# Attention and feed-forward sandwich on one core: one low sum behind the first exponentials, the last store on ScalarE's queue, two slices of the last block in other PSUM banks, and a new order of the engines' programs

## The chip, the core and the metric

The kernel runs on one core of a Trainium2 chip. Its engines run programs of their own and meet through semaphores: TensorE (PE; PEld is its weight load), VectorE (DVE), ScalarE (ACT), GpSimd (POOL), and SyncE (SP), which here only issues DMAs. The metric is the device time of one execution in microseconds (us); lower is better.

## What is computed

The input is x with 8 batches of 256 tokens of 128 features. Two residual steps follow each other, both with a layer norm ahead of and behind the inner function:

```
x = x + layernorm(attention(layernorm(x)))
x = x + layernorm(ffn(layernorm(x)))

attention: q, k, v = x Wqkv; softmax(q k^T / sqrt(128)) v          # one head of 128
ffn:       h = silu(x W1 * s1) * (x W2 * s2)                       # 128 -> 512
           h = gelu(h H1 * s3); h = gelu(h H2 * s4)                # 512 -> 512, twice
           y = h W3 * s5                                           # 512 -> 128
```

The weights of the ffn are -1, 0 or 1; s1 to s5 are scales of one output column each. All is float32.

## The kernel before

The 2048 tokens are 16 tiles of 128. They go through in five blocks of 2, 4, 4, 4 and 2 tiles (SIZES), blocks 0 to 4; the last is called LAST. Tokens stand along the free dimension in the ffn, so a slice (o = 0 to 3) is 128 of the 512 hidden features by all tokens of a block (256 or 512 columns).

**Steps of a block.** Attention: x_statistics, x_normalised (VectorE), x_transposes (TensorE), xT_copy; g_projection and scores (the product of q and k goes through one matrix "qk"); maxima (VectorE), exps (ScalarE, L382), probs_transposes (L1065), pT_copy, attend (L1081); then attention_out, x1_block, x1_normalised (VectorE). Each statistics step is followed by rsqrt on GpSimd (L315), which makes 1/std (rstd) of one of four norms, LN_X, LN_O, LN_X1, LN_Y. Ffn: x2_transposes; x2T_high (ScalarE) and x2T_low (VectorE) split the transposed input into a rounded high half and a low rest; up_high and up_low (L1121, L1128) are the two products with W1 and W2; silu (ScalarE) and gate (VectorE, L724) make the first activation; high and low (VectorE, L732, L621) split it. The layers are named A1, A2, A3 by the activation that they read: A1 multiplies by H1, A2 by H2, A3 by W3. gelu_high (L436) and gelu (L428) on ScalarE write the high half and the full activation of the next layer, low (VectorE) the low half. The last layer is followed by scaled_yT, y_transposes, y_statistics, y_shifts, y_normalised, last_add (GpSimd) and the store. The last block's last layer is written by another way: last_down (L1197), last_statistics (L770), rsqrt_last (L321), last_centred, last_out (L783), and a store per tile (L267).

**Begin and end.** A layer's products on TensorE are written as begin(layer, block, slices, early) and end(...): begin waits until the slices' PSUM banks are free (bank_free) and does the products of the first `early` input slices, high and low; end does the rest. high_terms and low_terms wait slice by slice for the high and low halves.

**PSUM.** There are eight banks, F0 to F3 and A0 to A3. The hidden layers write slice o into F[o]; up products of the last block use A0 to A3; attention uses the A banks (the F banks in block 0).

**Low sums and flags.** The weights are loaded twice, raw by SP (w12_raw, h1_raw, h2_raw, w3_raw) and rounded by a casting DMA of GpSimd (w12_hi, h1_hi, h2_hi, w3_hi; round_w12 and so on). low_sum(0) to low_sum(5) add up the low 16 bits of the raw weights to learn whether rounding lost anything: 0 (w12_raw) and 1 (h1_raw) on ScalarE (L461), 2 to 5 (h1_raw, h2_raw, h2_raw, w3_raw) on VectorE (L793). sum_flags (L993) sums them over partitions on TensorE, copy_flags (L799) puts the result into SBUF, and read_flag reads it into a register of TensorE, which decides at each slow_branch whether extra products are needed. With these weights they aren't. Flag 0 covers W1, W2 and half of H1, flag 1 the rest.

**What sets the order.** Each engine's program is a list of calls written out by hand at the end of its function: it runs its steps exactly in that order, and a step that waits holds up all behind it. SP's queue holds, in this order: x of block 0, the attention weights, x of block 1, the scales, x of block 2, w12_raw, h1_raw, h2_raw, x of block 3, w3_raw, x of block 4, then the stores. The lines that the change's first part touches, in ScalarE's list:

```
v_copy(0)
low_sum(0)
exps(0, 0)
xT_copy(1)
w3_row_copy()
gT_copy(1)
low_sum(1)
```

## Time and profile before

| | us |
|---|---|
| median of 3 runs | 131.22 (130.95 to 131.62) |
| the profiled execution | 130.89 |
| its span, from the first to the last instruction | 128.7 |
| TensorE busy | 121.8 (95%) |
| VectorE busy | 103.9 (81%) |
| ScalarE busy | 97.5 (76%) |
| GpSimd busy | 28.0 (22%) |

The spans are read on the slowest (here the only) core. A matmul's end is modelled, and matmuls overlap by some 0.16 us, so the start of a row's successor says more of the pace than a row's duration. The first 12 us and the last 4 us are where TensorE is least busy.

### The profile page before, as it was taken

The numbers are of one execution on the slowest core, as the hardware profiler recorded it, in microseconds if no ns is written. First come the engines' busy times: TensorE is split into PE (matmuls) and PEld (weight loads), VectorE is DVE, ScalarE is ACT, GpSimd is POOL, SyncE is SP. The second block draws the span as 40 slices with busy tenths as digits, with TensorE's granted clock in tenths as the row PEclk, the third lists the DMA queues.
The fourth block names the chain that finished last, engine by engine and source line by source line (L and its number), as shares of the span: only waits on it lengthen the run. The fifth ranks groups of instructions, "written<-read, shape, count | busy, mean of one in ns | idle before, by whom it ended". The sixth has DMA issues, their size and how long they took to land.

```text
span 128.7 us, 2354 instructions
## 1 busy us (share of the span) xinstructions
PE 121.8 (95%) x698; PEld 102.2 (79%) x698; DVE 103.9 (81%) x337; ACT 97.5 (76%) x182; POOL 28.0 (22%) x40
## 2 busy tenths in 40 slices
PE   7994999999999999999999999999999999999980
PEld 5582979999777988887889888888888778789970
DVE  1693789999998899966799999839999977696843
ACT  3237699987999929399999289799992996996520
POOL 3390330035300015410000084400002540000351
PEclk9999999999999999999999999999999999999999
DMA  4779999000300000000000001010000011000021
GB/s 105 234 248 399 383 376 341 21 0 8 81 0 5 0 0 8 0 0 0 5 0 0 0 5 41 26 58 3 0 5 0 0 44 43 0 5 0 0 76 52
DMA packets 5343, 8.28 MB, mean 64 GB/s; under 512 B 464, under 2 KB 2768, under 8 KB 5328
## 3 DMA queue, kind: packets, MB, share of 16 engines
q1 hardware_dynamic: 3984, 5.19, 12.5%
q0 software_dynamic: 1344, 2.88, 6.9%
q8 instruction: 10, 0.16, 0.5%
q14 instruction: 5, 0.04, 0.1%
HBM read 7.02 MB, written 1.05 MB: 63 GB/s over the span
## 4 chain that ended last, share of the span: by engine, by line
PE 79%; DMA 5%; ACT 5%; DVE 4%; issue 2%; SPq 2%; POOL 1%; POOLq 1%; ACTq 0%; DVEq 0%
PE F L1168 20%; PE F L1174 20%; PE A L1081 5%; PE A L1049 5%; DMA w_raw<-w 5%; PE F L1128 4%; PE F L1121 4%; PE A L1168 3%; PE A L1174 3%; PE A L1032 2%; PE A L1065 2%; PE A L1020 2%; ACT a_hi L436 2%; ACT act_full L428 1%; PE A L1209 1%
## 5 line engine op out<-in xcount | busy, mean ns | idle before, releaser
L315 POOL TENSOR_TENSOR rstd<-mv,minus_half 128x4 f32<-128x4 f32 (+1 forms) x19 | 18.4, 968 | 90.9 <-DVE mv L628 90.8
L1168 PE MATMUL F<-a_hi,h_hi 128*128 128x512 f32 (+1 forms) x160 | 37.1, 354 | 0.1
L1174 PE MATMUL F<-a_lo,h_hi 128*128 128x512 f32 (+1 forms) x160 | 36.4, 349 | 0.0
L621 DVE TENSOR_TENSOR a_lo<-act_full,a_hi 128x512 fp32r<-128x512 f32 (+1 forms) x52 | 31.1, 615 | 5.6 <-ACT act_full L428 4.5
L436 ACT ACTIVATE a_hi<-F,sc 128x512 fp32r<-128x512 f32 (+1 forms) x35 | 21.4, 625 | 13.5 <-PE F L1174 13.5
L1174 PEld LDWEIGHTS F<-a_lo,h_hi 128*128 128x128 f32 x160 | 26.7, 189 | 4.2 <-DVE a_lo L621 0.4
L1168 PEld LDWEIGHTS F<-a_hi,h_hi 128*128 128x128 f32 x160 | 26.3, 189 | 3.9 <-ACT act_full L428 0.5
L428 ACT ACTIVATE act_full<-F,sc 128x512 f32<-128x512 f32 (+1 forms) x40 | 24.0, 613 | 1.7 <-PE F L1174 1.7
L724 DVE SCALAR_TENSOR_TENSOR act_full<-F,sc,silu 128x512 f32<-128x512 f32 (+1 forms) x16 | 10.7, 677 | 0.6 <-ACT silu L417 0.5
L417 ACT ACT_TABLE_LOAD x8 | 10.3, 1283 | 0.1
L417 ACT ACTIVATE silu<-F,sc 128x512 f32<-128x512 f32 (+1 forms) x16 | 9.8, 634 | 0.5 <-PE F L1128 0.3
L1121 PE MATMUL F<-x2T_hi,w_hi 128*128 128x512 f32 (+1 forms) x32 | 10.1, 396 | 0.1
L1128 PE MATMUL F<-x2T_lo,w_hi 128*128 128x512 f32 (+1 forms) x32 | 9.4, 376 | 0.0
L628 DVE BATCH_NORM_AGGREGATE mv<-stats 128x2 f32<-128x9 f32 x62 | 8.1, 170 | 0.0
L732 DVE CAST a_hi<-act_full 128x512 fp32r<-128x512 f32 (+1 forms) x17 | 6.5, 392 | 1.2 <-ACT act_full L428 1.0
L631 DVE BATCH_NORM_STATS2 stats<-A 128x6 f32<-128x128 f32 x28 | 6.6, 277 | 0.0
L1121 PEld LDWEIGHTS F<-x2T_hi,w_hi 128*128 128x128 f32 x32 | 5.3, 189 | 1.3 <-issue 0.5
L1128 PEld LDWEIGHTS F<-x2T_lo,w_hi 128*128 128x128 f32 x32 | 5.5, 188 | 0.9
L631 DVE BATCH_NORM_STATS2 stats<-xs 128x6 f32<-128x128 f32 x16 | 3.8, 277 | 3.1 <-DMA xs<-x 3.1
L337 POOL TENSOR_TENSOR outs<-y_n,x 128x512 f32<-128x512 f32 (+1 forms) x4 | 4.6, 1160 | 5.7 <-ACT y_n L451 3.8
L644 DVE TENSOR_SCALAR xn<-x,mv,rstd 128x128 f32<-128x128 f32 x16 | 5.5, 404 | 0.3 <-POOL rstd L315 0.3
L684 DVE TENSOR_REDUCE neg_max<-A 128x2 f32<-128x512 f32 x7 | 4.7, 677 | 0.8 <-PE A L1049 0.7
(153 smaller groups left out, 192.0 us busy)
## 6 DMA issues: line engine op xcount, KB each, us to landing
h_raw<-h SPq DMA_DIRECT2D x2, 1024.0 KB, 11.5
h_hi<-h POOLq DMA_DIRECT2D x2, 1024.0 KB, 9.5
xs<-x SPq DMA_DIRECT2D x3, 256.0 KB, 3.6
out<-outs SPq DMA_DIRECT2D x3, 256.0 KB, 2.1
w_raw<-w SPq DMA_DIRECT2D x1, 512.0 KB, 6.2
w_hi<-w POOLq DMA_DIRECT2D x1, 512.0 KB, 7.7
xs<-x SPq DMA_DIRECT2D x2, 128.0 KB, 8.5
w_raw<-w SPq DMA_DIRECT2D x1, 256.0 KB, 15.7
```

The costliest lines, as they stand in the source:

```text
L315: nc.gpsimd.tensor_tensor(rstd[:, ln, tiles(b)], mv[:, ln, tiles(b), 1], minus_half[:, 0:SIZES[b]], ALU.pow).then_inc(rstd_ready[ln], 1)
L417: nc.scalar.activation(silu1[:, o % 2, c], up_banks(b, o)[0][:, c], ACT.Silu, scale=sc[:, S_W1 + o:S_W1 + o + 1]).then_inc(silu_ready, 1)
L428: nc.scalar.activation(act_full[:, o, c], F[o][:, c], ACT.Gelu, scale=sc[:, s:s + 1]).then_inc(a_full[n], 1)
L436: nc.scalar.activation(a_hi[n][:, o, c], F[o][:, c], ACT.Gelu, scale=sc[:, s:s + 1]).then_inc(a_hi_ready[n], 1)
L621: nc.vector.tensor_tensor(dst, full, hi.bitcast(f32), ALU.subtract).then_inc(done, 1)
L628: return nc.vector.bn_aggr(mv[:, ln, T0[b] + t, :], stats[:, ln, T0[b] + t, :])
L631: nc.vector.bn_stats(stats[:, ln, T0[b] + t, 0:6], tile(t)).then_inc(chain, 1)
L724: nc.vector.scalar_tensor_tensor(gated(b)[:, o, c], up_banks(b, o)[1][:, c], sc[:, S_W2 + o:S_W2 + o + 1], silu1[:, o % 2, c], ALU.mult, A ...
L1121: nc.tensor.matmul(bank, w_hi, x_hi, start=True, stop=False)
L1128: last = nc.tensor.matmul(bank, w_hi, x_lo, start=False, stop=True)
L1168: nc.tensor.matmul(out, terms[k][0], terms[k][2], start=(k == 0), stop=False)
L1174: last = [nc.tensor.matmul(out, terms[k][0], terms[k][3], start=False, stop=(k == KT - 1)) for out, terms in groups]
```

## The change

1. On ScalarE low_sum(0) moves behind exps(0, 0) and xT_copy(1). 2. The last tile's store moves from SP's queue to ScalarE's, with a semaphore of its own. 3. The last block's first two slices of layer A1 are written into A0 and A1 and no longer into F0 and F1; bank_free follows. 4. The five lists are in a new order; sums of work on each engine stay as they are.

```diff
+        def layer_bank(n, b, o):
+            if n == A1 and b == LAST and o < 2:
+                return A[o]
+            return F[o]
...
-            def store_last(t):
-                g, j = G0[LAST] + t // 2, t % 2
-                sp.wait_ge(last_ready, t + 1)
-                sp.dma_start(out_view[:, g, j * D:(j + 1) * D], outs[:, T0[LAST] + t, :]).then_inc(out_stored, 16)
+            def store_first_of_last():
+                sp.wait_ge(last_ready, 1)
+                sp.dma_start(out_view[:, G0[LAST], 0:D], outs[:, T0[LAST], :]).then_inc(out_stored, 16)
...
-            sp.wait_ge(out_stored, 16 * (LAST + SIZES[LAST]))
+            sp.wait_ge(out_stored, 16 * (LAST + 1))
+            sp.wait_ge(last_stored, 16)
...
             round_h1()
+            round_h2()
+            round_w3()
             rsqrt(LN_O, 0)
-            round_h2()
             rsqrt(LN_X1, 0)
             rsqrt(LN_O, 1)
             rsqrt(LN_X1, 1)
-            round_w3()
             rsqrt(LN_X, 3)
+            rsqrt(LN_X, 4)
             rsqrt(LN_O, 2)
             rsqrt(LN_Y, 0)
+            last_add(0)
             rsqrt(LN_X1, 2)
-            rsqrt(LN_X, 4)
             rsqrt(LN_O, 3)
             rsqrt(LN_Y, 1)
-            last_add(0)
...
-                nc.scalar.activation(act_full[:, o, c], F[o][:, c], ACT.Gelu, scale=sc[:, s:s + 1]).then_inc(a_full[n], 1)
+                nc.scalar.activation(act_full[:, o, c], layer_bank(n - 1, b, o)[:, c], ACT.Gelu, scale=sc[:, s:s + 1]).then_inc(a_full[n], 1)
...
+            def store_second_of_last():
+                act.wait_ge(last_ready, 2)
+                act.dma_start(out_view[:, G0[LAST], D:2 * D], outs[:, T0[LAST] + 1, :]).then_inc(last_stored, 16)
...
-            low_sum(0)
+            w3_row_copy()
             exps(0, 0)
             xT_copy(1)
-            w3_row_copy()
+            low_sum(0)
             gT_copy(1)
...
             y_statistics(0)
-            low(A2, 1, 0)
-            x1_block(2)
-            low(A2, 1, 1)
             low(A2, 1, 2)
             low(A2, 1, 3)
             y_shifts(0)
+            x1_block(2)
+            low(A3, 1, 0)
             x1_normalised(2)
...
             last_statistics(0)
+            last_statistics(1)
             last_centred(0)
-            last_statistics(1)
+            last_centred(1)
             last_out(0)
-            last_centred(1)
             last_out(1)
...
             def bank_free(n, b, slices):
                 if n == A1:
                     for o in slices:
-                        if b == LAST:
+                        if b == LAST and o < 2:
+                            pe.wait_ge(a_full[A1], KT * b + 3)
+                        elif b == LAST:
                             pe.wait_ge(a_full[A3], KT * (b - 1) + o + 1)
...
                 elif n == A2:
                     for o in slices:
                         pe.wait_ge(a_full[A2], KT * b + o + 1)
+                        if b == LAST and o < 2:
+                            pe.wait_ge(a_full[A3], KT * (b - 1) + o + 1)
```

**ScalarE in the head.** The rows are the start of its program, with the tensor that each writes and reads; low_bits from w12_raw is low_sum(0), the two act_full, sums rows are exps(0, 0). Before:

```order
L374 ACTIVATE act_full<-F1 128x256
L374 ACTIVATE act_full<-F2 128x256
L461 ACTIVATE low_bits,low_sums<-w12_raw 128x1024
L382 ACTIVATE act_full,sums<-F3,neg_max 128x256 x2
L374 ACTIVATE xT_odd<-A1 128x512
L475 ACTIVATE w3_row<-A3 128x128
L374 ACTIVATE gT_odd<-A1 128x512
L461 ACTIVATE low_bits,low_sums<-h1_raw 128x1024
```

And now:

```order
L475 ACTIVATE w3_diag<-ident,sc 128x128
L378 ACTIVATE act_full<-F2 128x256
L479 ACTIVATE w3_row<-A3 128x128
L386 ACTIVATE act_full,sums<-F3,neg_max 128x256 x2
L378 ACTIVATE xT_odd<-A1 128x512
L465 ACTIVATE low_bits,low_sums<-w12_raw 128x1024
L378 ACTIVATE gT_odd<-A1 128x512
L465 ACTIVATE low_bits,low_sums<-h1_raw 128x1024
```

The low sum has moved behind the exponentials and block 1's xT copy, and the small w3 steps stand elsewhere.

**TensorE around the second flag.** F0 and F1 from a1_hi and a1_lo are the first two slices of layer A1 of block 0; A2 from xT_even is scores(2, 1); the TENSOR_LOAD is read_flag. Before, the second one stood behind all of the layer's products:

```order
L993 MATMUL A1<-low_sums,ones 1x3
L1049 MATMUL A2<-xT_even,gT_even 128x256 x2
L1168 MATMUL F0<-a1_hi,h1_hi 128x256
L1168 MATMUL F1<-a1_hi,h1_hi 128x256
L1092 COMPARE_AND_BRANCH
...
L1174 MATMUL F3<-a1_lo,h1_hi 128x256 x4
L998 TENSOR_LOAD flags
L1168 MATMUL F0<-a2_hi,h2_hi 128x256
```

Now it stands ahead of the last input slice of the first two:

```order
L1002 MATMUL A1<-low_sums,ones 1x3
L1058 MATMUL A2<-xT_even,gT_even 128x256 x2
L1007 TENSOR_LOAD flags
L1181 MATMUL F0<-a1_hi,h1_hi 128x256
L1181 MATMUL F1<-a1_hi,h1_hi 128x256
L1101 COMPARE_AND_BRANCH
```

The read has moved some twenty products forward.

**VectorE ahead of the last block's first layer.** a1 rows are the last block's first activation (kept in pT_odd), a3 rows block 3's last; each CAST is high, each TENSOR_TENSOR is low. Before:

```order
L732 CAST a3_hi<-act_full 128x512
L621 TENSOR_TENSOR a3_lo<-act_full,a3_hi 128x512
L621 TENSOR_TENSOR a1_lo<-pT_odd,a1_hi 128x256
L732 CAST a1_hi<-pT_odd 128x256
L621 TENSOR_TENSOR a1_lo<-pT_odd,a1_hi 128x256
L621 TENSOR_TENSOR a3_lo<-act_full,a3_hi 128x512 x3
```

And now:

```order
L741 CAST a3_hi<-act_full 128x512
L741 CAST a1_hi<-pT_odd 128x256
L630 TENSOR_TENSOR a1_lo<-pT_odd,a1_hi 128x256
L630 TENSOR_TENSOR a3_lo<-act_full,a3_hi 128x512
L630 TENSOR_TENSOR a1_lo<-pT_odd,a1_hi 128x256
L630 TENSOR_TENSOR a3_lo<-act_full,a3_hi 128x512 x3
```

The first low half of block 3's last activation has moved behind one high and one low half of the last block. On ScalarE, gelu(A3, 3, 0), which the first CAST reads, now stands behind gelu_high(A3, 3, 1).

## Rows read from the trace of the kernel before

**Rows 1.** One stretch: length, busy us of each engine (instructions), PEclk, DMA share, GB/s.

```profile
38.00:50.00 12.00, 12.00 (x70) 10.18 (x69) 10.64 (x31) 9.16 (x15) 2.02 (x2) 1.00 0.01 3
```

**Rows 2.** TensorE's longest wait: engine, line, waited for: us in total, times, longest.

```profile
PE F L1065 <- ACT act_full L382: 1.6, 1, 1.6
```

**Rows 3.** The chain that ended last: start us, us, what.

```profile
3.10 6.22 DMA w_raw<-w
9.35 1.15 ACT low_bits L461 x2
...
28.23 0.14 ACT a_hi L436
...
37.69 1.16 PE A L1081 x8
```

**Rows 4.** In order of time, VectorE and ScalarE to 28 us: start, us, instruction [idle].

```profile
8.37 0.69 DVE L684 TENSOR_REDUCE neg_max<-F 128x2 f32<-128x512 f32 x1
...
10.41 0.46 ACT L382 ACTIVATE act_full<-F,neg_max 128x256 f32<-128x256 f32 x1
...
18.39 0.69 DVE L793 SCALAR_TENSOR_TENSOR low_pairs<-h_raw 128x512 bf16<-128x512 uint16 x1
...
19.00 0.14 DVE L799 TENSOR_REDUCE flags<-F 1x1 f32<-1x3 f32 x1
...
21.05 0.42 DVE L793 SCALAR_TENSOR_TENSOR low_pairs<-w_raw 128x256 bf16<-128x256 uint16 x1 [0.22 <-DMA w_raw<-w]
...
27.30 0.42 DVE L621 TENSOR_TENSOR a_lo<-act_full,a_hi 128x256 fp32r<-128x256 f32 x1
```

**Rows 5.** Line L276, the load of h2_raw: its issue, and its time to landing.

```profile
L276 SPq DMA_DIRECT2D h_raw<-h x1: 507/507/507, 4.1 to 4.1; - x1
...
DMA to landing us min/median/max: 14.2/14.2/14.2
```

**Rows 6.** In order of time, TensorE's weight loads and matmuls at two places.

```profile
19.82 0.42 PEld L1065 LDWEIGHTS A<-ident,probs_odd 128*128 128x128 f32 x4 [0.21 <-issue]
...
27.91 0.40 PE L1174 MATMUL F<-a_lo,h_hi 128*128 128x256 f32 x2
```

**Rows 7.** GpSimd's rsqrt(LN_O, 0), and its two h loads with the times to landing.

```profile
14.92 0.71 POOL L315 TENSOR_TENSOR rstd<-mv,minus_half 128x2 f32<-128x2 f32 x1 [5.24 <-DVE mv L628]
...
L305 POOL DMA_DIRECT2D h_hi<-h x1: 797/797/797, 8.9 to 8.9; - x1
L308 POOL DMA_DIRECT2D h_hi<-h x1: 778/778/778, 15.6 to 15.6; - x1
...
DMA to landing us min/median/max: 8.0/9.5/10.9
```

**Rows 8.** Near 104 us, VectorE and GpSimd in order of time; the page's group of L621.

```profile
104.12 1.32 DVE L621 TENSOR_TENSOR a_lo<-act_full,a_hi 128x512 fp32r<-128x512 f32 x1 [0.66 <-ACT act_full L428]
...
103.58 1.30 POOL L337 TENSOR_TENSOR outs<-y_n,x 128x512 f32<-128x512 f32 x1 [1.43 <-ACT y_n L451]
...
L621 DVE TENSOR_TENSOR a_lo<-act_full,a_hi 128x512 fp32r<-128x512 f32 (+1 forms) x52 | 31.1, 615 | 5.6 <-ACT act_full L428 4.5
```

**Rows 9.** Near 113 us, TensorE and VectorE in order of time.

```profile
111.80 1.07 PE L1174 MATMUL F<-a_lo,h_hi 128*128 128x512 f32 x4
113.00 0.95 PE L1168 MATMUL F<-a_hi,h_hi 128*128 128x256 f32 x6
...
113.71 0.42 DVE L621 TENSOR_TENSOR a_lo<-pT_odd,a_hi 128x256 fp32r<-128x256 f32 x1
```

**Rows 10.** The tail, VectorE, GpSimd and SP's queue in order of time.

```profile
125.21 0.29 DVE L770 BATCH_NORM_STATS2 stats<-F 128x6 f32<-128x128 f32 x1
...
125.81 0.60 POOL L321 TENSOR_TENSOR rstd<-mv,minus_half 128x1 f32<-128x1 f32 x1 [0.26 <-DVE mv L771]
...
126.02 1.15 SPq L267 DMA_DIRECT2D out<-outs  x2
```

**Rows 11.** The page: GB/s of all DMAs in 40 slices of 3.2 us.

```profile
GB/s 105 234 248 399 383 376 341 21 0 8 81 0 5 0 0 8 0 0 0 5 0 0 0 5 41 26 58 3 0 5 0 0 44 43 0 5 0 0 76 52
```

157 lines of the change are left out of this document (79 added, 78 removed).

## The prediction

> **What bounds the kernel now.** I read a table by stretch of time first, then what TensorE waited for, then the chain that ended last, and last the engines' own rows at the places where that chain leaves TensorE. In a stretch such as 38 to 50 us TensorE is busy all of the time, at full clock [rows 1]: there, instructions of other engines are hidden unless they come so late that TensorE has to stand. Time can be had at four places only. (1) The head: the longest wait of a matmul is 1.6 us, for the first exponentials (PE L1065 behind ACT L382) [rows 2]. The chain says why: w12_raw, issued at 3.10, lands 6.22 us later; only then does ScalarE's first low sum run, from 9.35 for 1.15 us [rows 3]; the exponentials stand behind it. (2) At 104 us products wait for a late low half (a_lo). (3) At 112.7 us the last block's first hidden layer stands until 113.00. (4) The tail behind TensorE's last matmul.
>
> **The head, step by step.** The maxima of batch 0 are ready at 8.37 + 0.69 = 9.06, but the exponentials start at 10.41, behind the low sum [rows 4]. Turned round, they start at about 9.1: 1.3 us earlier. TensorE also gets x_transposes(2) into the wait that is left, which saves it some 0.4 us behind. By its own list TensorE could be 1.7 us ahead. It doesn't keep this. VectorE's low_sum(3) reads h2_raw, which was issued at 4.1 and took 14.2 us to land [rows 5], so it lands at 18.3. In the trace of before low_sum(3) starts at 18.39 [rows 4], hardly later; after the change VectorE gets there sooner and stands until 18.3, and x2T_low(0), without which up_low(0, 0) can't run, is queued behind it. From there to low(A1, 0, 3), the step at 27.30 [rows 4], VectorE is full in both orders. It gains 18.39 to 18.32 (0.07), the 0.22 us wait for w3_raw at 21.05, as that sum moves back behind the first gates, and copy_flags(0), 0.14 us at 19.00, which moves ahead of the landing [rows 4]. Sum 0.43: low(A1, 0, 3) starts at 26.87.
>
> Then there is the second flag. read_flag(1) moves from behind all of A1's end groups to ahead of the first, right behind scores(2, 1). Before, many products were queued in TensorE when it read. Now all that is queued ends near 26.7, and copy_flags(1), which now comes behind high(A1, 0, 3), ends at about 26.75 too, just ahead of low(A1, 0, 3). What such a read costs is seen at the first flag: it was written at 19.00 + 0.14 = 19.14 [rows 4], and the next weights loaded at 19.82 after an idle 0.21 us with no engine named for it, "issue" [rows 6]. That is 0.68 us, the price I take. TensorE goes on at 26.75 + 0.68 = 27.43 with 2 high products (0.24), and at 27.67 come the 2 low ones that stood at 27.91 [rows 6]. So the first Gelu of layer 2, at 28.23 in the chain [rows 3], comes 0.24 earlier or a little more; I take 0.3. The range is 0.24 to 0.75: the latter if the read is hidden after all, for then VectorE's 0.43 and the 0.3 by which TensorE was later than VectorE here both count. From 28.23 to the attend at 37.69 [rows 3] the chain runs over ScalarE, VectorE and GpSimd in turn, through the same instructions in both orders: maxima(2, 1) only changes places with x_normalised(3), and the pT copy behind both comes no later. So the gain is handed on. **Head: -0.3 us.**
>
> **From 38 to 103 us.** I followed each moved step there to its use by TensorE. The closest are x1_block(2), now behind y_shifts(0) and so about 2 us later, whose normalised tiles come some 0.5 us before x2_transposes(2) wants them, and low(A1, 3, 3), with next to nothing to spare. No stall and no gain: **0**, range 0 to +0.4. On GpSimd the two weight loads (0.78 us for h2) fill part of the 5.24 us for which it idled before rsqrt(LN_O, 0) at 14.92 [rows 7]: 4 us of cover, cost 0. w3_diagonal behind gT_copy(0) is still ahead of its product: 0.
>
> **104 us.** gelu(A2, 3, 2) goes ahead of the four y_n. The low half made from it started at 104.12 and took 1.32 us, beside GpSimd's add of 1.30 us from 103.58; the mean of that line is 615 ns [rows 8]. Now two other low halves stand ahead of it and the add comes later too, since its y_n do, so that both start near 104.15: it ends between 104.8 and 105.5, and TensorE wants it near 105.4. Gain between 0.3 and 0; against it, x1_normalised(4) comes before a low half instead of behind it and waits for GpSimd's rstd, up to 0.1. **-0.1.**
> The Trainium skill (SBUF — State Buffer, Who interferes with whom) says that VectorE and GpSimd share a pair of ports which whoever starts first may hold for its whole instruction. By that rule the 1.32 us holds a wait, and the trace agrees. By it the moved last_add(0) could also hold up x1_block(2) or x1_normalised(2) by its whole length, some 0.8 us: TensorE would lose 0.3 us, and the sum below would be 0.6 instead of 0.9.
>
> **111 us.** The last 4 low products of layer 2 of block 3 start at 111.80; 4 of 0.23 end at 112.71. The next start at 113.00, when gelu(A3, 3, 1) has emptied F1 [rows 9]. In A0 and A1 they need only gate(4, 2), long done. Behind them 6 + 6 + 2 products of 0.12 lead to the low ones of the last slice at 114.39, for which low(A1, 4, 3) must be there; it ended at 113.71 + 0.42 = 114.13 [rows 9]. high(A3, 3, 0), ahead of it, now waits for a Gelu that stands second on ScalarE, one Gelu step or 0.6 us later; 0.3 to 0.4 of this is made good since low(A1, 4, 2) now runs where low(A3, 3, 0) stood waiting. So it ends at 114.3 to 114.45: just in time. Gain 0.29, and 0.06 for uneven starts after a stop: **-0.35**, range -0.4 to 0 (if VectorE is 0.35 late).
>
> **Tail.** The second tile's statistics start at 125.21 behind last_centred(0); now they start as soon as TensorE is done, at 125.05. Its rstd on GpSimd, at 125.81, then starts and ends 0.15 earlier, and last_out(1), which waits for it, starts 0.13 earlier [rows 10]. The store on ScalarE's queue buys nothing: SP's two issues lie within 126.02 to 127.17 [rows 10]; the second came due near 126.8, when the first had been handed over. What a first use of another queue costs is in no row; nearest is SP's issue itself, so I bound it at -0.1 to +0.35 and take 0. **-0.13.**
>
> **Sum**: -0.3 - 0.1 - 0.35 - 0.13 = -0.88. The profiled execution took 130.89 (span 128.7, and 2.2 around it): 130.0 after. The median of the runs is 131.22, 0.33 higher; medians are compared, so I forecast 131.22 - 0.9 = 130.3.
>
> **Rivals.** (a) *The flag's read is hidden*: -0.75 in place of -0.3, so 129.8. Against it: the 0.68 us at the first flag. (b) *A new stall in the middle, or a late low(A1, 4, 3)*, takes back 0.4 us or more: 130.7 to 131.2. For it: margins of 0 to 0.5 us at three places. (c) *The other side: the cast loads crowd out h2_raw.* The issue of h2_hi moves from 15.6 [rows 7] to 9.7 and w3_hi follows right behind, while h2_raw is under way, on whose landing VectorE hangs. They are 1.25 MB, 3.2 us at the 376 to 399 GB/s of those slices [rows 11]. If they are served side by side with h2_raw, it slips by s, up to 3.2 us, and the time is 130.3 + s: slower than before from s = 0.9, and 133.5 at the end. For it: between 10 and 22 us no bandwidth is left [rows 11]. Against it: the two h loads of GpSimd, issued at 8.9 and 15.6, took 10.9 and 8.0 us [rows 7], so the first lands at 19.8 and the second, which by then had been waiting, at 23.6: one after the other. h2_hi issued at 9.7 stands behind h1_hi as it did before.
> The Trainium skill (DMA: Bandwidth & Descriptors, Queues, rings and completion order) says that each DMA engine takes turns between queues, packet by packet, and starts the descriptors of one queue in order. By that rule h2_raw keeps its share whatever stands behind h1_hi, s is 0, and the sum stands; no trace here shows four such loads in one queue.
>
> **Chances.** Forecast 0.5 (130.3, own range 129.9 to 130.7), (a) 0.13, (b) 0.27, (c) 0.1. Some 0.66 us (0.5%) is what a measurement of this kernel can tell from none. Faster by more: (a) and most of the forecast's 0.5, 0.56. Slower by more: (c) beyond s = 1.6 and the worst of (b), 0.11. Same: 0.33. The range 129.5 to 131.5 holds (a), the forecast, (b), and (c) while s is small.
>
> **What would show it.** Exponentials of batch 0 at 9.1; VectorE idle until 18.3 before low_sum(3), ended by a DMA; TensorE idle for some 0.7 us near 27 us, named "issue"; first Gelu of layer 2 near 27.9; attend(2, 0) near 37.4; no matmul gap ahead of the last block's first layer. A landing of h2_raw past 19 us, or a TensorE wait over 0.3 us between 38 and 103, would prove me wrong.

## The result, and the profile after

| | before | changed |
|---|---|---|
| median of 20 runs each, us | 130.16 (129.68 to 131.62) | 129.91 (129.43 to 130.88) |
| profiled execution, us | 130.89 | 130.00 |
| its span, us | 128.7 | 127.8 |
| w12_raw, issue to landing in it, us | 6.2 | 6.4 |
| h2_raw, the same | 14.2 | 13.9 |

The ratio of the runs is 0.9943, with a 95% interval of 0.9919 to 0.9968: 0.42 to 1.05 us faster, at the middle 0.74 us. The means of the 20 runs stand 0.55 apart (130.45 and 129.91), the medians only 0.25, against the 0.9 forecast, for the reason below. The forecast was 130.3 us after a gain of 0.9; the gain of the two profiled executions is 0.89. Whether it exceeds 0.5% the interval doesn't settle. Runs above 132 us, with a granted clock of 0.98 to 0.99, are left out of all that follows, the profiled execution of the fourth kernel of experiment 3 among them.

**Two levels of time, which the three first runs hid.** The 20 runs of the kernel before are 11 between 129.68 and 130.19 us, and 9 between 130.73 and 131.62, with nothing between (in the later sets some runs fall into the gap). The three runs behind the 131.22 of the prediction are all of the upper group, and so is the profiled execution. Over all its runs of this study, the kernel before has 104 below 130.35 us (median 129.8) and 85 between 130.35 and 131.62 (130.9); a median between such groups tells of their shares. Of the changed kernel's 20 runs, 18 are below 130.35.

**The head.** In the changed kernel, in order of time, first the start of the chain that ended last, then VectorE's and ScalarE's instructions to 28 us (start, us, instruction, and in brackets the idle time before it and what ended it):

```profile
2.64 3.86 DMA xs<-x
...
8.69 0.60 DVE neg_max L693
```

```profile
9.32 0.47 ACT L386 ACTIVATE act_full<-F,neg_max 128x256 f32<-128x256 f32 x1 [0.38 <-DVE neg_max L693]
...
17.05 0.15 DVE L808 TENSOR_REDUCE flags<-F 1x1 f32<-1x3 f32 x1
17.99 0.69 DVE L802 SCALAR_TENSOR_TENSOR low_pairs<-h_raw 128x512 bf16<-128x512 uint16 x1 [0.21 <-DMA h_raw<-h]
...
26.21 0.14 DVE L808 TENSOR_REDUCE flags<-A 1x1 f32<-1x3 f32 x1
26.39 0.43 DVE L630 TENSOR_TENSOR a_lo<-act_full,a_hi 128x256 fp32r<-128x256 f32 x1
...
27.46 0.47 ACT L440 ACTIVATE a_hi<-F,sc 128x256 fp32r<-128x256 f32 x1 [0.49 <-PE F L1187]
```

The chain no longer begins with the landing of w12_raw [rows 3]: it begins with the x of the second group. The exponentials run at 9.32 in place of 10.41 [rows 4], and what is left before them is VectorE's maximum. low_sum(3) now stands until h2_raw has landed, as forecast, but at 17.99, not 18.3, since h2_raw took 13.9 us here in place of 14.2 [rows 5]. The idle time there is 0.21 us, and experiment 7 shows that nothing behind it would have come earlier without it. The first flag's copy, at 19.00 before, is at 17.05. The first Gelu of layer 2 comes at 27.46 in place of 28.23: 0.77 earlier, where 0.3 was forecast.

**The second flag and the middle.** TensorE's weight loads and matmuls of the changed kernel at five places:

```profile
26.73 0.30 PEld L1181 LDWEIGHTS F<-a_hi,h_hi 128*128 128x128 f32 x2 [0.21 <-issue]
...
36.85 1.16 PE L1090 MATMUL A<-v_even,pT_even 128*128 128x128 f32 x8
...
38.57 0.30 PEld L1130 LDWEIGHTS F<-x2T_hi,w_hi 128*128 128x128 f32 x2 [0.36 <-issue]
...
107.34 0.30 PEld L1130 LDWEIGHTS A<-x2T_hi,w_hi 128*128 128x128 f32 x2 [0.47 <-issue]
...
122.22 1.95 PE L1210 MATMUL F<-w_scaled,act_full 128*128 128x128 f32 x16
```

The flag's copy ended at 26.35 and the next weights are loaded at 26.73: 0.38 us, of which only 0.21 is idle, as products were still running at the copy's end; and not 0.68. attend(2, 0) starts at 36.85, 0.84 before the 37.69 of [rows 3]. TensorE's last products start at 122.22; before:

```profile
123.06 1.95 PE L1197 MATMUL F<-w_scaled,act_full 128*128 128x128 f32 x16
```

That is again 0.84. So from 37 to 122 us nothing was gained: 85.37 us lie between the two marks in both kernels. There were gains on the way, and they were spent. The loads at 38.57 (up_high(1, 3), which now waits for gate(1, 1)) and at 107.34 (up_high(4, 2)) stand 0.36 and 0.47 us where those of before stood 0 and 0.26. Most of the loss is early: attend(2, 1) starts 4.60 or 4.61 us after attend(2, 0) in the changed kernel, in all its profiles that have this order, and 4.43 to 4.45 in those with the old order.

GpSimd's last_add(0), which the change moves forward, meets a small instruction of VectorE, o_shift, that stood alone and took 0.15 us before:

```profile
53.78 0.74 POOL L341 TENSOR_TENSOR outs<-y_n,x 128x256 f32<-128x256 f32 x1 [2.47 <-ACT y_n L455]
53.81 0.73 DVE L713 TENSOR_TENSOR o_shift<-mv,rstd 128x4 f32<-128x4 f32 x1
```

It takes 0.73 us in seven of the ten profiles of kernels with the new order, and 0.15 in three, where the add takes 0.79 or 0.80 instead. In the first kind TensorE's load of x2T_hi near 59 us starts 22.64 to 22.66 us after attend(2, 0), in the second 22.54 to 22.58 (without the edit of up_high(1, 3)): some 0.1 us, which is still there at the last products (85.25 to 85.37 and 85.14 to 85.21).

**104 and 111 us.** VectorE and GpSimd near 104 us, then TensorE and VectorE near 112 us, in the changed kernel:

```profile
102.19 1.89 DVE L630 TENSOR_TENSOR a_lo<-act_full,a_hi 128x512 fp32r<-128x512 f32 x3
105.44 0.68 DVE L630 TENSOR_TENSOR a_lo<-act_full,a_hi 128x512 fp32r<-128x512 f32 x1
...
103.57 1.67 POOL L341 TENSOR_TENSOR outs<-y_n,x 128x512 f32<-128x512 f32 x1 [2.00 <-ACT y_n L455]
```

```profile
111.25 1.07 PE L1187 MATMUL F<-a_lo,h_hi 128*128 128x512 f32 x4
112.16 0.88 PE L1181 MATMUL A<-a_hi,h_hi 128*128 128x256 f32 x6
...
113.33 0.42 DVE L630 TENSOR_TENSOR a_lo<-pT_odd,a_hi 128x256 fp32r<-128x256 f32 x1
```

The low half of 1.32 us [rows 8] is gone: three take 1.89 together, and it is GpSimd's add that is now longer, 1.67 for 1.30. The high products of the last block's first layer follow the low ones of block 3's layer A2 without a stop, and its low half, which was to end between 114.3 and 114.45, ends at 113.75: VectorE wasn't late.

**The tail.** VectorE, GpSimd and the two queues, in the changed kernel:

```profile
124.21 0.30 DVE L779 BATCH_NORM_STATS2 stats<-F 128x6 f32<-128x128 f32 x1
...
124.15 1.23 POOL L325 TENSOR_TENSOR rstd<-mv,minus_half 128x1 f32<-128x1 f32 x2 [0.64 <-DVE mv L780]
...
125.51 0.34 SPq L271 DMA_DIRECT2D out<-outs  x1
...
125.80 0.37 ACTq L483 DMA_DIRECT2D out<-outs  x1
```

The second tile's rstd follows the first with no gap on GpSimd (0.26 us of idle before it in [rows 10]). last_out(1) ends at 125.76, 3.54 us after TensorE's last products began, where it was 3.73 before: 0.19 gained, 0.13 forecast. But from TensorE's last products to the end of the execution it is 7.78 us (7.76 to 7.78 in all nine profiles with the store on ScalarE's queue) after 7.83 (7.82 to 7.85 in the old order): only some 0.06 is left.

### The profile page after: what moved, and what is told of

Its sections match the earlier page's. It is cut to its first block, busy times and chain, and to the rows that moved or that the text cites. A ratio compares the mean times of both kernels' runs of the same rounds, so it can differ in the third digit from the quotient of the medians.

```text
span 127.8 us, 2356 instructions
## 1 busy us (share of the span) xinstructions
PE 122.6 (96%) x698; PEld 102.5 (80%) x698; DVE 103.3 (81%) x337; ACT 97.4 (76%) x182; POOL 27.9 (22%) x40
## 3 DMA queue, kind: packets, MB, share of 16 engines
q1 hardware_dynamic: 3840, 5.12, 12.6%
HBM read 7.02 MB, written 1.05 MB: 63 GB/s over the span
## 4 chain that ended last, share of the span: by engine, by line
PE 84%; DVE 6%; DMA 3%; ACT 1%; SPq 1%; issue 1%; DVEq 0%; ACTq 0%
PE F L1181 22%; PE F L1187 22%; PE A L1090 5%; PE A L1058 5%; PE F L1130 5%; PE F L1137 5%; PE A L1187 3%; PE A L1181 3%; DMA xs<-x 3%; PE A L1041 3%; PE A L1074 2%; PE A L1029 2%; DVE xn_odd L653 2%; PE F L1210 1%; PE A L1222 1%
## 5 line engine op out<-in xcount | busy, mean ns | idle before, releaser
L319 POOL TENSOR_TENSOR rstd<-mv,minus_half 128x4 f32<-128x4 f32 (+1 forms) x19 | 17.7, 935 | 87.1 <-DVE mv L637 87.0
L1181 PE MATMUL F<-a_hi,h_hi 128*128 128x512 f32 (+1 forms) x152 | 35.5, 355 | 0.0
L630 DVE TENSOR_TENSOR a_lo<-act_full,a_hi 128x512 fp32r<-128x512 f32 (+1 forms) x52 | 30.6, 602 | 5.9 <-ACT act_full L432 5.2
L1187 PE MATMUL F<-a_lo,h_hi 128*128 128x512 f32 (+1 forms) x152 | 34.9, 352 | 0.0
L440 ACT ACTIVATE a_hi<-F,sc 128x512 fp32r<-128x512 f32 (+1 forms) x33 | 20.5, 632 | 12.2 <-PE F L1187 12.2
L1187 PEld LDWEIGHTS F<-a_lo,h_hi 128*128 128x128 f32 x152 | 25.7, 189 | 4.0
L1181 PEld LDWEIGHTS F<-a_hi,h_hi 128*128 128x128 f32 x152 | 25.2, 189 | 3.6 <-issue 0.2
L432 ACT ACTIVATE act_full<-F,sc 128x512 f32<-128x512 f32 (+1 forms) x38 | 23.1, 621 | 1.7 <-PE F L1187 1.7
L341 POOL TENSOR_TENSOR outs<-y_n,x 128x512 f32<-128x512 f32 (+1 forms) x4 | 5.1, 1274 | 9.1 <-ACT y_n L455 6.9
```

The source lines that it names most:

```text
L319: nc.gpsimd.tensor_tensor(rstd[:, ln, tiles(b)], mv[:, ln, tiles(b), 1], minus_half[:, 0:SIZES[b]], ALU.pow).then_inc(rstd_ready[ln], 1)
L432: nc.scalar.activation(act_full[:, o, c], layer_bank(n - 1, b, o)[:, c], ACT.Gelu, scale=sc[:, s:s + 1]).then_inc(a_full[n], 1)
L440: nc.scalar.activation(a_hi[n][:, o, c], layer_bank(n - 1, b, o)[:, c], ACT.Gelu, scale=sc[:, s:s + 1]).then_inc(a_hi_ready[n], 1)
L630: nc.vector.tensor_tensor(dst, full, hi.bitcast(f32), ALU.subtract).then_inc(done, 1)
L1181: nc.tensor.matmul(out, terms[k][0], terms[k][2], start=(k == 0), stop=False)
L1187: last = [nc.tensor.matmul(out, terms[k][0], terms[k][3], start=False, stop=(k == KT - 1)) for out, terms in groups]
```

## Experiments

**1. The two kernels again, together on another chip.** No edit.

> The kernel before, once more, to see the spread of its own times and a second profile of it. Before's 20 times lie in two groups, 129.7 to 130.3 and 130.7 to 131.6; the profile that the prediction was built on is of the second (130.89). Theory (one level, the spread is the chip's): a second profile has the same gaps as the first (1.6 us before the first exponentials, 0.3 us at 113 us), whatever its time, and span 127.5 to 129. Rival (the gap at the head is itself variable, by the landing of w12_raw or h2_raw): in a profile with a time near 129.8 the first Gelu of layer 2 comes near 27.2, and in one near 130.9 near 28.2. Ratio to before 1.000, within 0.3%.

> The changed kernel, once more. Theory (the sum of the prediction, -0.9 us of 130 to 131): ratio 0.993. Rival (the true effect is the -0.25 us by which the two medians of 20 differ): ratio 0.998.

Before: median 129.98 us of 12 runs. Changed: 129.74 of 12, ratio 0.9974 (0.9941 to 1.0007). The profiled execution of before took 129.92 this time, 0.97 less than the first one of the same program. The load of w12_raw in it, its issue and its time to landing:

```profile
L274 SPq DMA_DIRECT2D w_raw<-w x1: 468/468/468, 3.1 to 3.1; - x1
...
DMA to landing us min/median/max: 4.8/4.8/4.8
```

and ScalarE and VectorE in it, in order of time:

```profile
7.91 1.06 ACT L461 ACTIVATE low_bits<-w_raw 128x1024 bf16<-128x1024 uint16 x1 [0.45 <-DMA w_raw<-w]
...
9.49 0.47 ACT L382 ACTIVATE act_full<-F,neg_max 128x256 f32<-128x256 f32 x1 [0.43 <-DVE neg_max L684]
...
17.50 0.69 DVE L793 SCALAR_TENSOR_TENSOR low_pairs<-h_raw 128x512 bf16<-128x512 uint16 x1
...
27.32 0.84 ACT L436 ACTIVATE a_hi<-F,sc 128x256 fp32r<-128x256 f32 x2 [0.61 <-PE F L1174]
```

The same load, issued at the same 3.1 us, lands 4.8 us later in place of 6.2 [rows 3]. The low sum is over before the maxima are, and the wait of 1.6 us [rows 2] isn't there: the exponentials wait for VectorE, low_sum(3) waits for nothing, and the first Gelu is 0.91 us earlier than in [rows 3]. So most of what the prediction calls the head's limit exists in one kind of execution only. Of the five profiles of kernels that keep VectorE's sums on their loads and before's order of VectorE and TensorE in the head (before twice, the two of experiment 2 and the first of experiment 3), the two with late landings lie in their kernel's upper group and the three with early ones in the lower. Over the 20 profiles taken for this study the load takes 4.5 to 4.9 us in 8 and 5.9 to 6.5 us in 12, never between, and h2_raw 11.4 to 12.6 us in the first and 13.4 to 14.4 in the second. With early landings the changed kernel gains less: its profile of this set (129.35 us; 4.5 and 12.6) is 0.57 below that of before, with attend(2, 0) 0.40 earlier and the last products 0.50.

But these 0.40 us aren't the change's. The exponentials start at 9.08 in this profile and at 9.49 in that of before, 0.41 apart, and from there to attend(2, 0) it is 27.29 and 27.28 us. In the 12 profiles whose chain begins with the load of the second group of x, the load takes 3.68 to 4.18 us and the exponentials start 2.82 or 2.83 us after its landing, whichever kernel it is. Two more profiles of the new order with early landings, in experiments 7 and 3, start the exponentials at 9.31 and 9.30 and take 130.04 (0.13 of it by its store) and 129.85 us, which is no less than the 129.67 to 129.92 of the old order with early landings (experiments 1, 2 and 3). Counted from the first exponential to the last products, the old order without a wait for w12_raw takes 112.52 to 112.78 us and the new one 112.50 to 112.83 (112.90 with late landings). So with early landings the change is worth some 0.1 us, and most of that is the tail.

**2. The banks alone, and the low sum alone.** The kernel before with layer_bank, which puts two slices of A1 of the last block into A's banks (as in the change's diff), and the kernel before with low_sum(0) behind xT_copy(1):

```
 exps(0, 0)
 xT_copy(1)
+low_sum(0)
```

> The kernel before with the last block's first two A1 slices in A0 and A1 (and what waits for these banks), and nothing else. Theory: the 0.3 us stop of TensorE before that layer goes, as in the changed kernel, so -0.3 us, ratio 0.998, and the matmuls there follow at 112.7. Rival: VectorE's low halves, which are in the old order here, are late and a stop of the same size stands a few products further on: 0.

> The kernel before with low_sum(0) behind exps(0, 0) and xT_copy(1) on ScalarE, and nothing else: all other orders are before's. Theory (VectorE hangs on the landing of h2_raw near 18.1): exponentials 1.1 to 1.3 us earlier, but low_sum(3) can start only 0.1 to 0.3 us earlier, so the first Gelu of layer 2 comes 0.2 to 0.4 us earlier, and the time is 0.3 us less, ratio 0.998. Rival (the head's 1.3 us is handed on whole): first Gelu near 27.0, ratio 0.991.

Banks: 5 runs at 129.09 to 129.38 and 7 at 130.05 to 130.68 us. Both levels of before, 129.46 to 130.2 and 130.72 to 131.28 beside it, have moved down by some 0.4 to 0.6 us. The median of 130.13 and the ratio of 0.9992 (0.9956 to 1.0027) hide that, since 7 of 12 runs fell in its upper group and only 12 of 34 of before's. Its TensorE rows, three marks in order of time:

```profile
37.46 1.16 PE L1086 MATMUL A<-v_even,pT_even 128*128 128x128 f32 x8 [0.19 <-DVE pT_even L665]
...
111.49 1.07 PE L1183 MATMUL F<-a_lo,h_hi 128*128 128x512 f32 x4
112.39 0.88 PE L1177 MATMUL A<-a_hi,h_hi 128*128 128x256 f32 x6
```

No stop at 112.4, as forecast, and the last products start at 122.38, 84.92 us after attend(2, 0), 0.45 less than in the first profile of either kernel and 0.37 to 0.45 less than in all with the old order (85.29 to 85.37). So the banks are worth some 0.4 us, a little more than the -0.35 of the prediction, and the new order of the middle takes nearly as much away (85.14 to 85.37 with both).

The low sum alone: 5 runs at 129.67 to 129.94, two at 130.21 and 130.40, 5 at 130.76 to 131.18; median 130.30, ratio 1.0025 (0.9989 to 1.0061). Both groups stay. Taking the load off the first exponentials isn't enough by itself.

**3. Are the loads the cause?** Six sums wait for loaded tiles. Their input is replaced by a constant tensor: for n = 0 only, for all six, for all six in the changed kernel, and for VectorE's four only. The flags then say nothing of the weights' low words.

```
-act.wait_ge(loaded, 16)
+act.wait_ge(zeroed, 4)
+half_words = spare.unsqueeze(1).to_broadcast([P, 8, P])
```

> The kernel before, in its old order, but low_sum(0) adds up the low bits of a constant tensor of ones (same columns, same engine) and waits for no load; so W1 and W2 are left out of the check for lost bits. Theory A (the two groups of before's times are two landings of the weight loads, about 7.9 and 9.3 us for w12_raw, and low_sum(0) hands on only the late one): the first low sum runs near 7.5 in every run and the exponentials at 9.5; in the late state low_sum(3) still waits for h2_raw (18.3), so 0.3 to 0.4 of the 0.9 us go and the upper group moves from 130.9 to 130.5 while the lower stays at 129.8. Rival B (the upper group comes from low_sum(0)'s wait alone): no upper group, all times 129.5 to 130.1, ratio 0.995. Rival C (the two groups have nothing to do with these loads): both groups stay, ratio 1.000.

> The kernel before, in its old order, with all six low sums on a constant tensor of ones, so no engine's program waits for a raw weight load except w3_scale near the end (the check for lost bits is left out altogether). Theory A: no upper group, 129.5 to 130.0 in all runs, since neither low_sum(0) nor low_sum(3) hands on a late landing; ratio 0.995 to 0.997. Rival C: both groups stay (130.7 to 131.2 in a third of the runs), ratio 1.000.

> The changed kernel with all six low sums on a constant tensor of ones (the check for lost bits is left out). Theory A: the changed kernel waits only for h2_raw before low_sum(3), by 0.2 us in the late state; its times go from 129.2 to 130.4 to 129.1 to 129.6, ratio 0.995 to before. Against e6 it then shows what the change is worth without any load in play: -0.3 to -0.5 us. Rival (the head's new order is worth 0.9 us by itself): 0.9 us under e6.

> The kernel before with the four sums that VectorE takes (n = 2 to 5) over a constant tensor in place of the loaded tiles; ScalarE's two (n = 0, 1) still wait for theirs. So the flags no longer stand for the tiles' words. Theory A (VectorE's sum over h2_raw, which ended at 18.39 us beyond the wait for the landing, and hangs back the second head's scores, makes the upper group): hardly any run above 130.5 us, median 129.8 to 130.0, as with all six sums off the loads. Theory B (the upper group comes from ScalarE's sums over w12_raw and h1_raw ahead of and behind the first exponentials): a third to two thirds of the runs stay at 130.6 to 131.4 us, and the median lies at 130.2 to 130.7. In a profile with the late landings A expects the first Gelu of layer 2 at 27.3 us, B at 27.9 or later.

With n = 0 off, 6 of 12 runs stay above 130.8; with VectorE's four off, 3 of 11 above 130.7 and two at 130.31 and 130.47 (of before, 20 of 35 beside it). With all six off, 10 of 12 are below 130.2 (median 129.88, ratio 0.9948, 0.9915 to 0.9981), and its profile shows late landings (6.0 and 13.4 us) beside early marks, in order of time:

```profile
9.32 0.47 ACT L382 ACTIVATE act_full<-F,neg_max 128x256 f32<-128x256 f32 x1 [0.78 <-DVE neg_max L692]
...
17.33 0.69 DVE L809 SCALAR_TENSOR_TENSOR low_pairs<-ones_sq 128x512 bf16<-128x512 uint16 x1
...
27.28 0.84 ACT L436 ACTIVATE a_hi<-F,sc 128x256 fp32r<-128x256 f32 x2 [0.61 <-PE F L1190]
```

27.28 is the 27.32 of an early execution. So late loads do no harm unless a sum waits for them, and the sum over w12_raw isn't the only one that does: without its wait the upper group stays. Whether ScalarE's two sums alone make one is less clear, since 3 to 5 of 11 is not much more than the 2 of 12 with all six off; what the first of them costs is seen in experiment 5. The changed kernel with all six off has a median of 129.79, 0.09 below: without late loads in play, the change is worth a tenth, as the profiles of experiment 1 say.

**4. The loads pushed later on purpose.** One more load, ahead of that of w12_raw:

```
+sp.dma_start(spare_raw[:, :], w3).then_inc(spare_loaded, 16)
 sp.dma_start(w12_raw[:, :], w12).then_inc(w12_loaded, 16)
```

> The kernel before with one more load, the 0.25 MB of w3 into a tile that nobody reads, on SP's queue ahead of w12_raw's. At the 376 to 399 GB/s of the head that is 0.7 us, by which w12_raw, h1_raw and h2_raw land later. Theory A (late landings make the upper group, and each 0.1 us of lateness beyond 7.9 us at w12_raw costs 0.1 us): the lower group goes away; all runs above 130.3 us, median 130.9 to 131.7. Theory B (the groups have another cause, and the landings only go with it): both groups stay where they are, 129.5 to 130.2 and 130.5 to 131.6 us.

> The changed kernel with the same further load of 0.25 MB ahead of w12_raw's. Theory A (the changed kernel has the first exponentials off the load and waits for h2_raw alone, which costs it little up to a landing at 18.3 us): median 129.9 to 130.6 us, 0.2 to 0.8 above that without the load, and 0.7 us or more below that of the kernel before with the same load. Theory B (the lateness costs both the same): it stays 0.2 to 0.4 us below the kernel before with the same load, in a profile with the same landings.

Before with it: one run at 130.21, the ten others from 130.54 to 131.74, median 130.91 us, where the kernel before had 17 of 22 below 130.35 beside it. The lower group is gone. ScalarE in its profile:

```profile
9.76 1.06 ACT L465 ACTIVATE low_bits<-w_raw 128x1024 bf16<-128x1024 uint16 x1 [2.23 <-DMA w_raw<-w]
10.82 0.46 ACT L386 ACTIVATE act_full<-F,neg_max 128x256 f32<-128x256 f32 x1
```

The changed kernel with it: 130.22, 0.69 lower, 8 of 12 below 130.35. This settles that late landings raise the time of before, and that the changed kernel bears them better. It isn't immune: 4 runs lie at 130.83 to 131.77, and its profiled one (131.16) was late from wa_raw on, which took 3.25 us to land.

**5. Single moves of the head undone or made alone.** In the changed kernel: low_sum(0) ahead of the first exponentials; copy_flags(0) behind low_sum(3); low_sum(4) right behind low_sum(3); up_high(1, 3) behind up_low(1, 2); and that together with low_sum(3) behind pT_copy(1, 0). As diffs to the changed kernel, in this order:

```
+low_sum(0)
 exps(0, 0)
 xT_copy(1)
-low_sum(0)
...
-copy_flags(0)
 x1_normalised(0)
 low_sum(3)
+copy_flags(0)
...
 low_sum(3)
+low_sum(4)
 x2T_low(0)
 pT_copy(1, 0)
-low_sum(4)
...
-up_high(1, 3)
 up_low(1, 2)
+up_high(1, 3)
...
-low_sum(3)
 x2T_low(0)
 pT_copy(1, 0)
+low_sum(3)
```

> The changed kernel with low_sum(0) back ahead of the first exponentials. Theory A (the move behind the exponentials is what took the upper group away): an upper group comes back, a third or more of the runs at 130.2 to 131.0 us, median 129.9 to 130.3. Theory B (the move is worth next to nothing by itself, and the new order of the second head's work took the upper group away): median 129.7 to 129.9, no run or one above 130.3. In a profile with the late landings the exponentials begin at 10.3 us under both, and the first Gelu of layer 2 at 27.9 to 28.2 under A, 27.5 under B.

> The changed kernel with copy_flags(0) back behind low_sum(3) on VectorE, where a late h2_raw holds it. Theory A (the first flag's copy behind the sum over h2_raw is the second of two waits that make the upper group: TensorE can't read the flag until it is copied): with h2_raw landing late the copy is at 19.0 us and the first Gelu of layer 2 at 27.9 to 28.2 us, as in the kernel before; a third or more of the runs at 130.3 to 131.0 us, the median 129.9 to 130.4. Theory B (the sum's own wait matters, not what stands behind it; the changed kernel has the same wait): median 129.7 to 129.9 us, first Gelu at 27.4 to 27.6.

> The changed kernel with low_sum(4) back between low_sum(3) and x2T_low(0) on VectorE. Theory A (what matters is only that the flag's copy is ahead of the late sum): median 129.7 to 129.9 us as without the edit. Theory B (0.68 us of low_sum(4) ahead of x2T_low(0), on which up_low(0, 0) waits, is what binds, and more so when h2_raw is late): the head comes 0.5 to 0.7 us later in a profile with the late landings, median 130.1 to 130.5 us.

> The changed kernel with up_high(1, 3) behind up_low(1, 2) again, as in the kernel before. In the changed kernel's trace its weights load after an idle 0.36 us at 38.2 to 38.6, since it waits for gate(1, 1), which ends at 38.46. Theory: that stop goes (up_low(1, 2) stands in it), 0.2 us less at the attend of 41.6 and at the end, time of e2 less 0.2 us. Rival: TensorE's stop only moves on to up_high(1, 3) behind: 0.

> The changed kernel with up_high(1, 3) back behind up_low(1, 2), and with low_sum(3) behind x2T_low(0) and pT_copy(1, 0) on VectorE, so that a late h2_raw holds back one read of a flag and nothing else at the head. Theory A (what is left of h2_raw's landing is on the path in the changed kernel): the head gains 0.2 to 0.5 us in the profile with the late landings and 0 to 0.2 with the early ones, median 129.4 to 129.6 us. Theory B (the flag's read then comes later and takes the gain back, since low_sum(3) has to end before copy_flags(1) and moves by the 1 us of the two copies): median 129.7 to 129.9 us, the same as without the edit.

| edit to the changed kernel | median us | ratio to before (95%) | first Gelu of layer 2 in the profile | the same, counted from the first exponential |
|---|---|---|---|---|
| none (20 runs, and 12) | 129.91, 129.74 | 0.9943, 0.9974 | 27.46, 26.98 | 18.14, 17.90 |
| low_sum(0) ahead | 130.75 | 1.0027 (0.9990 to 1.0064) | 28.28 | 17.72 |
| copy_flags(0) behind | 131.04 | 1.0069 (1.0041 to 1.0098) | 29.02 | 19.46 |
| low_sum(4) ahead | 130.54 | 1.0026 (0.9995 to 1.0057) | 28.00 | 18.36 |
| up_high(1, 3) behind | 129.68 | 0.9920 (0.9892 to 0.9948) | 27.61 | 18.30 |
| that, and low_sum(3) behind | 130.43 | 0.9992 (0.9959 to 1.0026) | 28.06 | 18.79 |

All profiles but the 26.98 have the late landings. By the medians, three moves are each worth 0.6 to 1.3 us here, though low_sum(0) made alone in the kernel before was worth nothing. In the profiles, low_sum(4) costs 0.22 us from the first exponential on; the rest of its later Gelu is a later x. The lowest runs of the three, 130.10, 130.59 and 130.04 us, lie above the changed kernel's medians: either nearly all of their runs were late, or the moves also count when the loads land early. No early profile of them was taken, so this stays open. low_sum(0) back, ScalarE:

```profile
9.51 1.06 ACT L465 ACTIVATE low_bits<-w_raw 128x1024 bf16<-128x1024 uint16 x1 [0.74 <-DMA w_raw<-w]
10.56 0.45 ACT L386 ACTIVATE act_full<-F,neg_max 128x256 f32<-128x256 f32 x1
```

The exponentials are 1.24 us later than in the changed kernel and the Gelu 0.82. copy_flags(0) back, VectorE and TensorE:

```profile
18.11 0.69 DVE L802 SCALAR_TENSOR_TENSOR low_pairs<-h_raw 128x512 bf16<-128x512 uint16 x1 [0.34 <-DMA h_raw<-h]
18.73 0.14 DVE L808 TENSOR_REDUCE flags<-F 1x1 f32<-1x3 f32 x1
...
19.47 0.41 PE L1097 MATMUL F<-ident,xn 128*128 128x128 f32 x2 [1.36 <-DVE flags L808]
```

The flag is stuck behind the sum that waits for h2_raw, and TensorE, whose x2_transposes(0) stand behind read_flag(0) in the new order, stands 1.36 us for it; 0.57 us pass from the copy's end at 18.87 to TensorE's next weight load at 19.44. With low_sum(3) behind pT_copy(1, 0), two sums follow one another at 19.66 and 20.46 just ahead of the gates:

```profile
19.66 0.68 DVE L802 SCALAR_TENSOR_TENSOR low_pairs<-h_raw 128x512 bf16<-128x512 uint16 x1
...
20.46 0.69 DVE L802 SCALAR_TENSOR_TENSOR low_pairs<-h_raw 128x512 bf16<-128x512 uint16 x1
...
21.78 0.47 PE L1130 MATMUL F<-x2T_hi,w_hi 128*128 128x256 f32 x2 [0.69 <-DVE act_full L733]
```

TensorE waits 0.69 us for the bank that the gate empties. Theory B of that run, which saw the flag's read as what would take the gain back, was wrong in place and too mild; so was A. up_high(1, 3) back shows the 0.36 us at 38.57 gone and attend(2, 1) 4.50 us after attend(2, 0) in place of 4.61, in both kernels with this edit: 0.11 us. At the last products the distance is 85.22, within the 85.14 to 85.37 of the eight profiles without the edit, and the median is 0.06 to 0.23 below. It is the lowest of all kernels run, though no measurement here parts it from the changed kernel. With low_sum(3) at 18.37 after 0.60 us of waiting (h2_raw took 14.2 us), its first Gelu is 27.61, 0.15 behind the changed kernel's: that is what is left of the landing's price at 18.3, and at 17.99 nothing is left (experiment 7).

**6. The flag's copy made early in the kernel before, alone and with low_sum(0) behind exps(0, 0).** As a diff to the kernel before:

```
+copy_flags(0)
 x1_normalised(0)
 low_sum(3)
-copy_flags(0)
...
-low_sum(0)
 exps(0, 0)
+low_sum(0)
 xT_copy(1)
```

> The kernel before with one line moved: copy_flags(0) ahead of x1_normalised(0) and low_sum(3) on VectorE. low_sum(0) still stands ahead of the exponentials and waits for w12_raw. Theory A (either wait alone makes the upper group): both groups stay, 129.6 to 130.1 and 130.4 to 131.3 us, each with a third of the runs or more. Theory B (the flag's copy alone makes it): hardly a run above 130.4 us, median 129.8 to 130.0.

> The kernel before with two lines moved: copy_flags(0) ahead of x1_normalised(0) and low_sum(3) on VectorE, and low_sum(0) behind the first exponentials on ScalarE. Theory A (these two waits make the upper group, and nothing else is needed to take it away): at most two runs above 130.4 us, median 129.7 to 130.0, first Gelu of layer 2 at 27.1 to 27.6 us whether the loads land early or late. Theory B (the rest of the new order is needed, low_sum(4) and the second flag's read above all): a third of the runs or more stay above 130.4 us, median 130.1 to 130.7.

Medians 131.00 and 131.46, ratios 1.0052 (1.0018 to 1.0087) and 1.0079 (1.0037 to 1.0122): both slower, against both theories. Both profiles have early landings and are late all the same. In the first, VectorE stands for TensorE's sum of the flags, whose weights are loaded at 17.52 us in the old order and at 16.82 in the changed kernel, for all its late landings:

```profile
17.75 0.15 DVE L799 TENSOR_REDUCE flags<-F 1x1 f32<-1x3 f32 x1 [0.99 <-PE F L993]
```

In the second, low_sum(0) stands directly behind the exponentials, one place ahead of where the change puts it, and holds up xT_copy(1) for which TensorE's projections wait:

```profile
10.05 1.05 ACT L461 ACTIVATE low_bits<-w_raw 128x1024 bf16<-128x1024 uint16 x1
11.09 0.59 ACT L374 ACTIVATE xT_odd<-A 128x512 f32<-128x512 f32 x1
...
11.73 1.13 PE L1020 MATMUL A<-xT_odd,qk 128*128 128x512 f32 x2 [0.86 <-ACT xT_odd L374]
```

That place is my edit's, not the change's, so this run doesn't test whether the two moves would do; it tells what one place costs: on the chain the next scores (L1049) start at 13.75 us, 0.76 later than with the sum behind xT_copy(1) (12.99, experiment 2), though the exponentials started 0.18 earlier.

**7. The last store back on SP's queue.**

```
-act.dma_start(out_view[:, G0[LAST], D:2 * D], outs[:, T0[LAST] + 1, :]).then_inc(last_stored, 16)
+sp.dma_start(out_view[:, G0[LAST], D:2 * D], outs[:, T0[LAST] + 1, :]).then_inc(last_stored, 16)
```

> The changed kernel with the store of the last tile's second half back on SP's queue, behind the first half's. Theory A (the prediction's tail: the two stores one behind the other on SP cost 0.3 us between the issue of the first and that of the second, of which 0.05 to 0.13 us show at the end): median 0.05 to 0.3 us above that of the changed kernel, 129.8 to 130.1 us, and the time between the last arithmetic and the end 0.1 to 0.3 us longer. Theory B (both lie under the same wait for the DMA's completion): no difference, within 0.1 us, 129.7 to 129.9.

Median 129.95 us, ratio 0.9961 (0.9932 to 0.9990), in another set of runs than the changed kernel's own 129.91 and 129.74. SP's queue in its profile:

```profile
125.43 0.34 SPq L271 DMA_DIRECT2D out<-outs  x1
125.82 0.43 SPq L290 DMA_DIRECT2D out<-outs  x1
```

The second store is issued at 125.82, on ScalarE's queue at 125.80, but its arithmetic was over 0.07 us earlier here (last products at 122.14): it had to stand behind the first. From the last products to the end of the execution it is 7.90 us, where the nine profiles with the store on ScalarE's queue have 7.76 to 7.78. So the queue is worth 0.13 us, which the medians of different sets of runs can't show: Theory A, at the low end of its range.

This profile has early landings (4.6 and 12.5 us), and beside the changed kernel's first one it settles what the late h2_raw costs there. ScalarE and VectorE, in order of time:

```profile
9.31 0.47 ACT L388 ACTIVATE act_full<-F,neg_max 128x256 f32<-128x256 f32 x1 [0.60 <-DVE neg_max L694]
...
17.68 0.69 DVE L803 SCALAR_TENSOR_TENSOR low_pairs<-h_raw 128x512 bf16<-128x512 uint16 x1
18.76 0.42 DVE L631 TENSOR_TENSOR x2T_lo<-F,x2T_hi 128x256 fp32r<-128x256 f32 x1 [0.38 <-ACT x2T_hi L380]
...
27.46 0.47 ACT L442 ACTIVATE a_hi<-F,sc 128x256 fp32r<-128x256 f32 x1 [0.49 <-PE F L1188]
```

The exponentials start at the same time, low_sum(3) doesn't wait, 0.31 us earlier than with the late landing, and the first Gelu comes at the same 27.46. What is behind low_sum(3) waits for x2T_high on ScalarE, not for VectorE.

## Why the prediction was wrong where it counted, and what held

The time lay 0.4 us below the forecast, inside the range. The gain in the two late executions came out as summed, but by terms that missed in opposite directions, which is luck:

| term | forecast | late landings (first two profiles) | early landings (experiment 1) |
|---|---|---|---|
| head, to attend(2, 0) | -0.3 | -0.84 | -0.40 |
| of it, to the first exponentials | -1.3 | -1.09 | -0.41, by x's landing |
| middle, 104 us and banks, to the last products | 0 - 0.1 - 0.35 | 0.00 | -0.10 |
| tail and the rest of the execution | -0.13 | -0.05 | -0.07 |
| sum | -0.88 | -0.89 | -0.57 |

**The step that failed first: the level.** "The profiled execution took 130.89 ... The median of the runs is 131.22 ... I forecast 131.22 - 0.9": the sum was read from an execution with late landings and set off from three runs of the same kind, as if the kernel had one time and each execution had the wait of 1.6 us before the first exponentials. The runs showed a median of 130.16 before the change and of 129.91 after it, 0.25 apart. Set off from the groups, a gain of some 0.1 with early landings and of 0.9 with late ones gives 129.8 - 0.1 = 129.7 and 130.9 - 0.9 = 130.0; the changed kernel's 18 lower runs go from 129.43 to 130.16. So the change takes the upper group away and hardly moves the lower one. Experiments 1, 3 and 4 show the cause: w12_raw and h2_raw land at two levels, some 1.5 us apart, under the same program.

**Head: the exponentials came as forecast, the limit behind them didn't.** They start at 9.32, against some 9.1. "It doesn't keep this", since VectorE hangs on h2_raw, was the second step that failed: of the 1.09 us, 0.84 are kept at attend(2, 0), and the landing takes none of them away. low_sum(3) did wait, for 0.21 us, but the same kernel without that wait has its first Gelu at the same 27.46 (experiment 7); only at 18.37 does the wait cost something, 0.15 us (experiment 5). low(A1, 0, 3) started at 26.39, where 26.87 was forecast; with h2_raw at 18.3 as forecast it started at 26.54, so 0.15 of it is the landing and 0.33 I can't place. The second flag was priced at 0.68 us, the distance at the first flag, and took 0.38. At the first, TensorE was in its v projection when the flag was written (8 products from 18.74 us for 1.06), so the distance held other work; the idle time was 0.21 in both rows [rows 6]. Its weight loads went on at 26.73, where 27.43 was forecast: 0.4 from the earlier end of the copy, 0.3 from the read. Of these 0.70 us, 0.54 reached attend(2, 0). What I had not seen is that the move of copy_flags(0), booked at its own 0.14 us, is a condition for the rest: put back alone, it costs some 1.2 us (experiment 5), because in the new order TensorE's transposes stand behind the read.

**The middle: right that nothing stands for long, wrong that it costs 0.** The range "0 to +0.4" held it. The banks bring some 0.4 alone (experiment 2) and the whole middle 0.00 to 0.15; the difference, 0.2 to 0.45 by the profiles, is the price of the new order between 38 and 109 us. 0.17 of it is there at attend(2, 1), behind the stop at 38.57, of which undoing one move gave back 0.11; some 0.1 is the meeting of last_add(0) with o_shift; the load at 107.34 stands 0.21 us longer. The prediction had taken up that last_add(0) could hold up VectorE for its whole length, at x1_block(2) or x1_normalised(2), and left it out of its sum; it did so at the instruction between them, for 0.58 us, and TensorE lost 0.1 and not 0.3. "A TensorE wait over 0.3 us between 38 and 103" was to prove the prediction wrong, and the 0.36 us at 38.57 are such a wait. Rival (b), a new stall in the middle of 0.4 us or more, was nearly what happened, hidden by the head's surplus in the late pair.

**104 us.** The wait that named a_lo is gone and up_high(4, 2) spent it. VectorE's low halves are short beside a longer add of GpSimd, so which of the two gets longer has turned round.

**Rival (c)**, the cast loads crowding out h2_raw: false. With h2_hi and w3_hi issued from 9.7 us on, h2_raw took 13.9 us, against 14.2 [rows 5], and 12.6 against 12.3 with early landings.

**Tail.** 0.19 us by the last arithmetic for 0.13, of which 0.05 are left at the end of the execution. The store's queue, taken as 0, is worth 0.13 (experiment 7): without it the new order of the last statistics would have ended 0.07 later than before (7.90 us after 7.83), for a reason that the traces don't show.

**Left open.** What makes a run's loads land early or late: nothing in the traces before 3.1 us differs that I could name, and the share of late runs of the kernel before went from 5 in 22 to 22 in 34 between sets of runs, which were taken on different chips (on one chip, 20 in 35 and 13 in 32). Whether the three moves of experiment 5 also cost time when the loads land early. Not tried: the changed kernel's head with the old order of the middle and the banks. By the two ledgers (85.14 to 85.37 us between the marks, 84.92 with the banks alone) it should be 0.2 to 0.45 us below the changed kernel, and it would be the next kernel to run.
